# Dispatch scatters in groups of four, each group waited for

## The reference

```python
top_w, top_idx = jax.lax.top_k(probs, TOP_K)                  # 8 of 160 experts for each token
combine = combine.at[jnp.arange(T)[:, None], top_idx].set(top_w)
h1 = jax.nn.silu(jnp.einsum('th,eih->eti', x, w_gate))
h1w = h1 * combine.T[:, :, None]
routed = jnp.einsum('eti,ehi->th', h1w, w_down)
shared = jax.nn.silu(x @ w_gate_shared.T) @ w_down_shared.T
```

## Time and profile before

| | before |
|---|---|
| timed runs, median (lowest to highest) | 903.72 us (902.05 to 905.78) |
| profiled execution, span from first to last instruction | 1049.1 us |
| PE busy | 806.3 us (77%) |
| DVE busy | 493.2 us (47%) |
| ACT busy | 381.5 us (36%) |
| POOL busy | 356.9 us (34%), of which dispatch scatters 127.1 us, x128 |
| DMA | 207.45 MB, mean 198 GB/s |
| stages by the trace | attention 0 to 340, mix 340 to 655, experts 655 to 1000, combine to 1049.1 us |

### The profile page before, as it was taken

How to read it: one execution, slowest core, us unless ns; L and a number is a source line. 1 busy time by engine, 2 the same in 40 slices (tenths; PEclk the granted TensorE clock), 3 DMA queues, 4 the chain that set the end, 5 groups by cost and what they waited for, 6 DMA issues and landing times. The chain is left out here.

```text
span 1049.1 us, 14869 instructions
## 1 busy us (share of the span) xinstructions
PE 806.3 (77%) x3800; PEld 528.4 (50%) x3800; DVE 493.2 (47%) x1287; ACT 381.5 (36%) x809; POOL 356.9 (34%) x360
## 2 busy tenths in 40 slices
PE   8989999999868888297493210988888787898395
PEld 4644444444345656174262110766666665666274
DVE  1677777777142585256432941322222222322077
ACT  2247777767724334215111000233333333333101
POOL 9101011110000014635356470355555555555400
PEclk9989999999969989799597655888889998988799
DMA  6998777786511113311122135788888888886296
GB/s 229 316 334 267 262 258 270 274 278 232 186 45 44 37 52 107 118 65 74 58 78 98 55 110 180 244 272 273 262 268 266 278 267 249 269 266 204 91 422 254
DMA packets 103410, 207.45 MB, mean 198 GB/s; under 512 B 25863, under 2 KB 51505, under 8 KB 97088
## 3 DMA queue, kind: packets, MB, share of 16 engines
q1 hardware_dynamic: 64160, 128.94, 37.1%
q10 hardware_dynamic: 24320, 42.74, 12.4%
q0 software_dynamic: 14880, 35.17, 9.2%
HBM read 117.76 MB, written 96.08 MB: 204 GB/s over the span
## 5 line engine op out<-in xcount | busy, mean ns | idle before, releaser
L1738 POOL DMA_INDIRECT contributions<-c_c,e_dest x182 | 177.0, 973 | 183.2 <-ACT c_c L1719 123.4
L1886 POOL DMA_INDIRECT row_pool<-rows,places x128 | 127.1, 993 | 213.0 <-issue 155.3
L1693 DVE COPY e_xt<-e_psx 128x256 f32<-128x256 f32 (+1 forms) x130 | 67.5, 530 | 251.2 <-PE e_psx L1625 100.5
L541 DVE TENSOR_REDUCE a_mx<-a_psS 128x2 f32<-128x1024 f32 x128 | 152.0, 1218 | 30.8 <-PE a_psS L363 30.5
L1639 PE MATMUL e_psg<-e_xt,e_w 128*128 128x64 f32 (+2 forms) x676 | 134.9, 338 | 34.2 <-ACT e_g L1712 26.4
L499 ACT ACTIVATE a_e<-a_psT 128x512 f32<-128x512 f32 x256 | 135.5, 600 | 57.9 <-PE a_psT L393 51.6
L1639 PEld LDWEIGHTS e_psg<-e_xt,e_w 128*128 128x128 f32 x676 | 108.3, 218 | 45.1 <-issue 33.0
L1712 ACT ACTIVATE e_g<-e_psg 128x128 f32<-128x128 f32 (+1 forms) x130 | 42.2, 324 | 241.4 <-PE e_psg L1639 143.8
L1650 PE MATMUL e_psy<-e_w,e_g 128*128 128x256 f32 (+1 forms) x442 | 119.7, 435 | 10.8 <-ACT c_c L1719 6.2
L1719 ACT ACTIVATE c_c<-e_psy,e_weight 128x256 f32<-128x256 f32 x182 | 80.7, 475 | 72.9 <-PE e_psy L1650 30.3
L1625 PE MATMUL e_psx<-m_c,rows 128*128 128x128 f32 x364 | 69.9, 303 | 43.1 <-PEq L676 36.7
(11 more groups left out here) (284 smaller groups left out, 951.4 us busy)
## 6 DMA issues: line engine op xcount, KB each, us to landing
row_pool<-fill SPq DMA_DIRECT2D x32, 1260.0 KB, 7.2
e_w<-w ACTq DMA_DIRECT2D x156, 256.0 KB
rows<-row_pool SPq DMA_DIRECT2D x143, 140.0 KB
c_c<-contributions SPq DMA_DIRECT2D x16, 1024.0 KB, 17.3
a_k<-k_parts SPq DMA_DIRECT2D x64, 128.0 KB, 3.3
rows<-row_pool SPq DMA_DIRECT2D x78, 70.0 KB
a_q<-q_parts SPq DMA_DIRECT2D x32, 128.0 KB, 4.2
a_q<-q_parts SPq DMA_DIRECT2D x64, 64.0 KB, 3.4
```

The source lines that it names most:

```text
L541: nc.vector.tensor_reduce(mx[:, at.slot, qt, 2 * DH * pair::HALF], psS[:, pair], AX, ALU.max).then_inc(maxed, 1)
L1693: nc.vector.tensor_copy(XT[:, at.slot % XT_RING, 0:n], ps_x(at, 0, n)).then_inc(xt_done, 1)
L1738: nc.gpsimd.indirect_dma_start(out=contrib, out_offset=bass.IndirectOffsetOnAxis(ap=dest[:, result(f) + k:result(f) + k + 1], axis=0), in_ ...
L1886: nc.gpsimd.indirect_dma_start(out=pool, out_offset=bass.IndirectOffsetOnAxis(ap=place[:, b, t, k:k + 1], axis=0), in_=rows[:, b, t], in_o ...
```

## The change

Before the first of every four scatters, except the first four of a batch, POOL waits until every scatter of this batch issued so far has landed. `before` is what `sent[0]` holds already from batch 0 when batch 2 uses it. 28 waits are added in all, 7 in each batch; no instruction is taken away and none moves past another.

```diff
+RUN = 4
...
         def dispatch(b, sent, tiles):
 
+            before = 0 if b == B - 1 else b // 2 * TT * TOP_K
             for t in tiles:
                 for k in range(TOP_K):
+                    if k % RUN == 0 and t * TOP_K + k > 0:
+                        nc.gpsimd.wait_ge(sent, 16 * (before + t * TOP_K + k))
                     nc.gpsimd.indirect_dma_start(
                         out=pool, out_offset=bass.IndirectOffsetOnAxis(ap=place[:, b, t, k:k + 1], axis=0),
                         in_=rows[:, b, t], in_offset=None, bounds_check=POOL_ROWS - 1,
```

## The result

The changed kernel takes 945.29 us (median of 4 runs, 943.67 to 946.44). The kernel before, run beside it, takes 904.75 us (902.05 to 905.79). The ratio is 1.0443, with a 95% interval of 1.0422 to 1.0464: 40.5 us slower. The forecast was +22.5 us, 926, with a range up to 942. So the direction and the place were right, and the size was not.

The account below looks back on a forecast made before the run. Without holds POOL has no spare time, so 28 waits of 1.6 us, less those hidden in batch 0, make SP wait 26.2 us for the dispatch; less 3.7 regained, +22.5 on 903.7 gives 926 us, range 912 to 942.

Parts of the forecast that it names:

- What bounds the kernel: Mix without holds: batches may start at 52.3, 105.4, 148.3 us; POOL has no spare time; SP asks at 193.6.
- holds: Signals arriving up to 16 us after the work, beside scatters; 64.6 us in mix, taken to belong to the traced execution alone.
- What one wait costs: POOL between groups of four scatters: 1.6 us for each wait, bounds 0.5 and 2.8.
- Batch 0's two hidden waits: The wait inside tile 0 and the one ahead of tile 1 vanish in the 20.8 us before tile 1 may start.
- The relief of 3.7 us: First row load to PE's first matmul: 3.3 us instead of 7.05, with the weights long in; a gain of 3.7.
- SP before: In the kernel before, SP is ready for rows at 193.6 us, the dispatch complete at 191.6, 2.0 us earlier.
- Let through: Rival: holds are in every execution and the pauses in POOL's scatters shorten them; -27.6 us, 876; chance 0.15.
- hidden: Rival: SP is ready 59.6 us after the last batch's start, the dispatch landed at 54.1; 904 us; chance 0.09.
- Absorbed: Rival: batches 0 to 2 absorb their waits, only batch 3 counts; +8.8 less 3.7, 909 us; chance 0.13.
- Doesn't wait: Rival: the added waits don't wait for the landings they name, a threshold being met early; given no chance.
- the period of the fours: Sign in POOL's trace: about 2.9 us from the fourth scatter's start to the next instead of 1.31.
- the shrinking span: Sign: the profiled span may shrink while the timed run grows, showing that trace and timed run differ by the holds.

Follow-up runs that it names:

- the run with one entry's rows: Kernel before, but SP issues only the first entry's rows in mix, those of entries 1 to 4 at the beginning of experts: 904.32 us, ratio 0.9998.
- the three-batch run: Changed kernel with the waits by fours in batches 0 to 2 alone (21 waits), last batch without: 928.01 us, ratio 1.0250 against the kernel before.

## Why the prediction was right in direction and wrong in size

**What bounds the kernel.** Right: a run without holds, POOL without spare time, lateness handed from batch to batch, SP as the one who waits for the dispatch. `rows_done` in the changed kernel allows the starts about 52.6, 106.0 and 149.4 us after the first scatter (DVE's last writes for them end at 438.90, 492.40 and 535.70, and POOL took 0.7 to 1.0 us from there to a scatter in the kernel before); worked out of a trace with 64.6 us of holds in mix they were 52.3, 105.4 and 148.3. From the first scatter to SP's first row load the two profiles of the kernel before differ by 258.3 - 195.9 = 62.4 us, so the 64.6 was a good reckoning. SP has the weights issued after 192.1 us (193.6 forecast). Wrong was the reason given, that holds come with the profile. The page that I leaned on there, the Trainium skill, NOTIFIC — the notification-queue block, section 7.1, allows an engine to be stalled on the way of its trace records; but ten profiles were taken and only one has holds, so being traced is not enough, and no run shows whether that block had a part in the one.

**What one wait costs.** This is the step that failed: "2.1 + 0.8 - 1.3 = 1.6 us for each wait". The bounds, 0.5 and 2.8, held the truth; the value did not. I had taken the landing from the last slice of traffic, 2.0 to 2.1 us after the start, but the count moves later: the landing has a median of 2.5 us in every profile that shows it, with and without waits. A plain wait is an idle time of 2.27 in place of 0.30, so 1.97 us. The formula of the Trainium skill (DMA: Bandwidth & Descriptors, Anatomy of one DMA — SWDGE (gpsimd) path) gave a landing of 2.3 us by estimate and a wait of 1.8; the measured landing is 2.5, so it was nearer than my row, and still short.

And not all waits are plain. The 27 waits that end on a landing have 67.8 us idle before them; the first (3.55) hides under the gate of tile 1. For the other 26, (67.8 - 3.55) - 26 x 0.30 = 56.5 us, or 2.17 each, against 26 x 1.6 = 41.6. That is 14.9 us of the miss: 26 x 0.37 = 9.6 from the plain price, 3.6 from the one wait beside the weights, and the rest, 1.7, from the others: 0.85 of it from the wait of 3.12 in batch 1, beside which SP issues no load, and 0.3 from one of 2.56 (444.83) just behind the load of 437.77. On the weights the Trainium skill has a sentence (DMA: Bandwidth & Descriptors, SWDGE vs HWDGE vs iDMA): within a DMA engine the queues that GpSimd and SP feed are different ones and take turns. The run with the weights behind the rows agrees, in that the longest landing falls from 6.1 to 3.6 us; the turns themselves no run here shows.

**Batch 0's two hidden waits.** Right: tile 1 starts 20.77 us after the first scatter, released by m_x2t, 20.8 forecast. That this gate costs the changed kernel little, 1.7 us, I had not seen.

**The relief of 3.7 us.** Wrong, in two ways. PE is released by the end of the mix block, which SP reaches only after nine row loads, so it starts 7.06 us after the first load whether the weights are long in or not. And a sooner start would have gained nothing, as the run with one entry's rows shows.

**SP before.** I had the dispatch landed 2.0 us ahead of SP. In fact SP waits 4.2 us for the last scatters, which land beside the weights, and its row load comes at 195.9 instead of 193.6. That takes 2.3 us off the loss. In this place something did come back: the last scatter of the changed kernel lands long after the weights, and from its start to SP's row load it is 2.7 us instead of 5.8. Both are in the sum below.

**The sum again.** 22.5 forecast; +14.9 for the waits; +3.7 for the relief; -2.3 for SP before; +0.7 between POOL's end and SP's load (1.8 us instead of 1.1); +2.4 for scatters that issue a little slower without any wait (POOL ends at 236.0; less the 56.5 of waits that is 179.5, where the forecast had 218.7 - 41.6 = 177.1; 0.9 of this is one pause of 1.17 us at 598.33, for which the profile shows no wait). Together 41.9, against 41.8 in the traces and 40.5 timed.

**The rivals.** *Let through* and *hidden* needed holds in every execution; there are none. *Absorbed* fell with the three-batch run. *Doesn't wait* is refuted by 27 waits that end on a landing. Of the signs I named, the period of the fours (2.9 forecast, 3.23 to 3.36 seen at 20 of the 27 waits, longer at the others) gave the price's error at once; the shrinking span, 1049.1 to 943.1, was no sign of anything, since the first span was not that kernel's usual one.

## What to carry to other kernels

On an engine without spare time a wait for a landing costs the whole way from issue to landing and back to the next issue, less one issue (here 2.5 + 0.8 - 1.3 = 2.0 us); price it by the moment at which the waiting engine is released, not by the last bytes on the DMA engines, and price apart the waits that fall beside other loads. Here waiting one group further back was free where waiting for the group just issued cost 40 us. When a profiled execution is far from the timed runs, profile the kernel again before explaining the difference.

## What the runs showed of the hardware that was not expected

- The same kernel gave one execution with a span of 1049.1 us, with signals held up to 16 us beside the scatters, and one of 902.9 us without any.
- A scatter of 128 rows lands 2.4 us after its start at the least and 2.5 in the median, waited for or not; beside 13 weight loads of 256 KB it took up to 6.1 us in the changed kernel.
- The time from SP's first row load to the end was 318.1, 318.2 and 318.0 us in three kernels, although in one of them PE began 4 us sooner; with the weights behind the rows it was 325.0.
